# Bias of a fused adapter kernel as 32 rows of the slot products, and the first weight chunk in two transfers

## What is computed

```
y    = x @ W.T + b + 2 * (x @ A[slot].T) @ B[slot]
base = y @ W_base.T + b_base
top2, sel = top_k(y @ W_router.T, 2);  w = softmax(top2) spread over the 8 experts
h    = y @ A_e.T  for every expert e (rank 16)
out  = x + base + 2 * sum_e w_e * (h_e @ B_e)
```

## Time and profile before

| what | value |
|---|---|
| median of three executions | 66.52 us |
| the profiled execution, time | 66.64 us |
| the profiled execution, span from first to last instruction | 64.9 us |
| TensorE matmuls, busy | 61.1 us (94%), 422 matmuls |
| VectorE busy | 36.9 us (57%) |
| ScalarE busy | 22.9 us (35%) |
| GpSimd busy | 17.1 us (26%) |
| granted TensorE clock, mean over the span | 1.0 of full |
| read from memory, written | 7.37 MB, 2.10 MB |

### The profile page before, as it was taken

The page is one execution under the profiler, slowest core; times in us unless marked ns, Lnnn a source line. Parts: engine busy times, 40 slices in busy tenths (PEclk is TensorE's granted clock), DMA queues, the critical chain, the costliest instruction groups (busy, mean ns, idle before and its releaser), DMA issues.

```text
span 64.9 us, 1174 instructions
## 1 busy us (share of the span) xinstructions
PE 61.1 (94%) x422; PEld 60.2 (93%) x422; DVE 36.9 (57%) x105; ACT 22.9 (35%) x46; POOL 17.1 (26%) x29
## 2 busy tenths in 40 slices
PE   5989999999999999999999999999999999999920
PEld 5969999999999999989999999999999999999910
DVE  0057959999899685126805675012768255956040
ACT  0669078606999898054121100020201131020000
POOL 6700000000799997759360000011000000000000
PEclk9999999999999999999999999999999999999999
DMA  0899998303899305155659997500044000033513
GB/s 0 222 358 353 402 407 267 115 5 96 225 316 374 128 6 130 37 130 126 146 90 399 351 375 282 200 0 0 0 171 154 9 0 0 0 121 121 229 48 127
DMA packets 6025, 10.57 MB, mean 163 GB/s; under 512 B 755, under 2 KB 2547, under 8 KB 6020
## 3 DMA queue, kind: packets, MB, share of 16 engines
q1 hardware_dynamic: 5730, 10.17, 47.1%
q10 hardware_dynamic: 290, 0.33, 1.5%
HBM read 7.37 MB, written 2.10 MB: 146 GB/s over the span
## 4 chain that ended last, share of the span: by engine, by line
PE 89%; DMA 4%; ACT 1%; DVE 1%; DVEq 0%; issue 0%
PE ps L693 26%; PE ps L601 23%; PE ps L705 19%; PE ps L753 8%; PE ps L662 5%; DMA wt<-w_chunks 4%; PE ps L728 2%; PE ps L733 2%; PE ps L739 1%; PE ps L716 1%; ACT wt_hi L352 1%; DVE xn L554 1%; DVEq L71 0%; PE ps L672 0%
## 5 line engine op out<-in xcount | busy, mean ns | idle before, releaser
L693 PE MATMUL ps<-am,x_hi 128*128 128x384 f32 x64 | 16.6, 340 | 0.0
L705 PE MATMUL ps<-bm,x_hi 128*128 128x280 f32 x64 | 13.0, 297 | 0.0
L693 PEld LDWEIGHTS ps<-am,x_hi 128*128 128x128 f32 x64 | 11.4, 188 | 0.0
L693 PE MATMUL ps<-am,x_lo 128*128 128x384 f32 x32 | 10.8, 338 | 0.0
L319 POOL TENSOR_TENSOR x_lo<-xt,x_hi 128x512 fp32r<-128x512 f32 x8 | 10.8, 1361 | 0.0
L705 PEld LDWEIGHTS ps<-bm,x_hi 128*128 128x128 f32 x64 | 10.1, 189 | 0.0
L705 PE MATMUL ps<-bm,x_lo 128*128 128x280 f32 x32 | 9.3, 290 | 0.0
L554 DVE TENSOR_TENSOR xn<-ps,xn 128x280 f32<-128x280 f32 (+1 forms) x16 | 6.1, 418 | 2.7 <-PE ps L753 2.6
L601 PE MATMUL ps<-wt_hi 128*128 128x280 f32 (+1 forms) x32 | 7.0, 316 | 0.2 <-ACT wt_hi L352 0.2
L601 PE MATMUL ps<-wt_lo,wt_hi 128*128 128x280 f32 (+1 forms) x32 | 7.0, 314 | 0.0
L326 POOL CAST am<-as_hl 128x128 fp32r<-128x128 f32 x8 | 2.9, 373 | 14.1 <-PE ps L693 14.1
(11 more groups left out here) (74 smaller groups left out, 99.4 us busy)
## 6 DMA issues: line engine op xcount, KB each, us to landing
xt<-x_t SPq DMA_DIRECT2D x4, 512.0 KB, 6.5
xn<-x_n SPq DMA_DIRECT2D x4, 512.0 KB, 5.5
out_n<-xn SPq DMA_DIRECT2D x7, 256.0 KB, 2.1
wt<-w_chunks SPq DMA_DIRECT2D x2, 582.0 KB, 6.2
g_st<-g_hl SPq DMA_DIRECT2D x12, 81.0 KB, 2.1
ab<-adapters SPq DMA_DIRECT2D x8, 64.0 KB, 2.7
wt<-w_chunks SPq DMA_DIRECT2D x1, 326.0 KB, 4.2
wt<-w_chunks SPq DMA_DIRECT2D x2, 128.0 KB, 3.0
```

The source lines that it names most:

```text
L693: last = mm(a_bank(b)[:, 0:R + WA], v[:, p, i, tok], am[:, i, level, at:at + R + WA], start=(i == 0 and n == 0), stop=False, skip_group_ch ...
L705: mm(b_bank(b)[:, 0:QB], v[:, p, i, tok], bm[:, i, level, :], start=(i == 0 and n == 0), stop=False, skip_group_check=True)
```

## The change

1. Chunk 0 comes in two transfers: SP's queue brings all 512 stationary columns, ScalarE's queue all 652 moving ones. ScalarE rounds the stationary columns in two instructions of 256; VectorE's rounding of columns 0 to 255 is gone, and its remainder of the 512 stationary columns stands ahead of that of the last 368 moving ones. TensorE does all four high x high products of the first 280 columns, and then the four high x low ones.
2. The two matmuls with the ones are gone, and with them the matrix of ones, its rounding on GpSimd, and both splits around them. `bsum` is summed over partitions further: 64 rows to 32 (with `b_base`, which comes as row 0 of a 32-row input padded with zeros), 32 rows in place, then a transfer moves rows 16 to 31 to partitions 0 to 15 (`moved`), and VectorE adds them (`folded`). Sixteen rows are left; they are split in high and low, and stand as rows 96 to 127 of `g_st`, which now has 128 rows. Two transfers bring them for pair 0 ahead of the rest, two for the pairs 1 to 3.
3. Pair 0 (and 2) has banks 2 and 3 for `routed` and 4 and 5 for `plain`, pair 1 (and 3) banks 0 and 1, 6 and 7. Block 0's first products wait for the remainders of M row block by row block, not for all.
4. Order: `slots_routed(0)` stands behind `routed(3)`; `weighted_transpose(0)` behind `plain(1)`, no longer next to `stack_transpose(1)`; `plain(2)` ahead of the experts of blocks 0 and 1; ScalarE and VectorE follow (`stack_t(1)` ahead of `weighted_hi(0)`, `stack(1)` ahead of `choose(0)`).
5. The rounding of `x` for pairs 2 and 3 is in two instructions per pair and not in one.

```diff
-W0_PIECES = [slice(D // 2, D), slice(0, D // 2), slice(D, D + QB), slice(D + QB, CB)]
+W0_PIECES = [slice(0, D), slice(D, CB)]
-GK = CROW + 4
+GK = CROW + 2 * NC
...
-            for n in (0, 1):
-                sp.dma_start(wt[:, 0, W0_PIECES[n]], w[:, 0, W0_PIECES[n]]).then_inc(w0_in[n], 16)
+            sp.dma_start(wt[:, 0, W0_PIECES[0]], w[:, 0, W0_PIECES[0]]).then_inc(w0_in[0], 16)
...
-            sp.wait_ge(bb_hi_done, 1)
-            spread(CROW, bb_hl[:, 0:1, :])
-            sp.wait_ge(bb_lo_done, 1)
-            spread(CROW + 1, bb_hl[:, 1:2, :])
+            sp.wait_ge(quarter_done, 2)
+            sp.dma_start(moved, bsum[NC:QP]).then_inc(moved_in, 16)
...
-                    sp.wait_ge(c_hi_done, 2)
-                    sp.wait_ge(c_lo_done, 2)
+                    for i, ready in enumerate((c_hi_done, c_lo_done)):
+                        sp.wait_ge(ready, 1)
+                        sp.dma_start(g_st[CROW + i * NC:CROW + (i + 1) * NC, 0, :].bitcast(F32),
+                                     c_hl[:, i, :].bitcast(F32)).then_inc(gst_in[0], 16)
                     for i in range(2):
-                        spread(CROW + 2 + i, c_hl[:, i:i + 1, :])
+                        sp.dma_start(g_st[CROW + i * NC:CROW + (i + 1) * NC, 1:PAIRS, :].bitcast(F32),
+                                     c_hl[:, i:i + 1, :].bitcast(F32).to_broadcast([NC, PAIRS - 1, WC])
+                                     ).then_inc(cst_in, 16)
...
-            for n in (2, 3):
-                act.dma_start(wt[:, 0, W0_PIECES[n]], w[:, 0, W0_PIECES[n]]).then_inc(w0_in[n], 16)
+            act.dma_start(wt[:, 0, W0_PIECES[1]], w[:, 0, W0_PIECES[1]]).then_inc(w0_in[1], 16)
             act.wait_ge(w0_in[0], 16)
-            for i in (2, 3):
-                c = slice(i * P, (i + 1) * P)
+            for c in (slice(D // 2, D), slice(0, D // 2)):
                 hi(wt_hi[:, 0, c], wt[:, 0, c]).then_inc(w0_hi_done, 1)
...
+                if i == 2:
+                    dve.wait_ge(bbase_in, 16)
+                    dve.wait_ge(halves_done, 1)
+                    nc.vector.tensor_tensor(upper[0:QP], bsum[QP:HP], bb[QP:HP], ALU.add).then_inc(quarter_done, 1)
+                    dve.wait_ge(quarter_done, 1)
+                    nc.vector.tensor_tensor(bsum[0:QP], bsum[0:QP], upper[0:QP], ALU.add).then_inc(quarter_done, 1)
...
+            dve.wait_ge(moved_in, 16)
+            nc.vector.tensor_tensor(bsum[0:NC], bsum[0:NC], moved, ALU.add).then_inc(folded, 1)
...
-            for s, c in enumerate(COLS):
-                last = mm(ps[:, C_BANK + s, 0:c.stop - c.start], ones_r[:], bsum_st[:, c], start=True, stop=True)
-            last.then_inc(c_done, 1)
...
+                    if b == 0 and i != 1:
+                        pe.wait_ge(m_lo_done, 2 * max(i + 1, 2))
...
             routed(2, range(2, KB))
+            routed(3)
             slots_routed(0)
-            routed(3)
             plain(0)
-            weighted_transpose(0)
             stack_transpose(1)
             plain(1)
+            weighted_transpose(0)
             slots_plain(0)
             slots_plain(1)
             slots_routed(1)
+            plain(2)
             experts_block(0)
             experts_block(1)
-            plain(2)
```

More of the change, by code:

```diff
@@ L48 @@
 CB = CH + 4
+QP = HP // 2
+NC = (P - 6 * R) // 2
 NT = NE + NE * R
@@ L115, in build @@
         hw_flat = hw[:].rearrange("p a t c -> p (a t c)")
-        upper, bb = hw_flat[0:HP, 0:WC], hw_flat[HP:HP + 1, 0:WC]
+        upper, moved = hw_flat[0:HP, 0:WC], hw_flat[0:NC, 0:WC]
         hw_hi = sb("hw_hi", [P, NB, P], F32R)
@@ L120, in build, with first_a, first_b @@
         ident = sb("ident", [P, P])
-        ones = sb("ones", [P, P])
-        ones_r = sb("ones_r", [P, P], F32R)
         iota = sb("iota", [P, NE])
         ps = ctx.enter_context(nc.psum_tensor("ps", [P, 8, 512], F32))
-        G_BANK, C_BANK = 0, 2
-        def first_bank(p):
-            return 0 if p % 2 else 4
+        G_BANK = 0
+        def first_a(p):
+            return 0 if p % 2 else 2
+        def first_b(p):
+            return 6 if p % 2 else 4
         def a_bank(b):
-            return ps[:, first_bank(b // 2) + b % 2, :]
+            return ps[:, first_a(b // 2) + b % 2, :]
         def b_bank(b):
-            return ps[:, first_bank(b // 2) + 2 + b % 2, :]
+            return ps[:, first_b(b // 2) + b % 2, :]
         def x_rounded(p, n):
-            return 2 * p + n + 1 if p < 2 else 3 + p
+            return 2 * p + n + 1
         def rt_at(b):
@@ L301, in _ @@
             nc.gpsimd.memset(ident[:], 0.0).then_inc(id_zero, 1)
-            nc.gpsimd.memset(ones[:], 1.0).then_inc(const, 1)
             nc.gpsimd.memset(h_stack[:], 0.0).then_inc(id_zero, 1)
@@ L311, in _ @@
                            allow_small_or_imprecise_dtypes=True).then_inc(const, 1)
-            pool.wait_ge(const, 1)
-            nc.gpsimd.tensor_copy(ones_r[:], ones[:]).then_inc(ones_rounded, 1)
             def x_split(p, n):
@@ L374, in x_high @@
                 act.wait_ge(x_in[p], 16)
-                step = 2 if p < 2 else KB
-                for k in range(0, KB, step):
-                    hi(x_hi[:, p, k:k + step, :], xt[:, p, k:k + step, :]).then_inc(x_hi_done, 1)
+                for k in range(0, KB, 2):
+                    hi(x_hi[:, p, k:k + 2, :], xt[:, p, k:k + 2, :]).then_inc(x_hi_done, 1)
             w_high(1)
@@ L418, in weighted_hi @@
                 hi(hw_hi[:, 2 * p:2 * p + 2, :], a_scratch(p)).then_inc(hw_hi_done, 1)
-            for p in range(PAIRS):
+            stack_t(0)
+            shares(0)
+            stack_t(1)
+            weighted_hi(0)
+            shares(1)
+            weighted_hi(1)
+            for p in range(2, PAIRS):
                 stack_t(p)
@@ L491, in _ @@
                 lo(g_hl[:, 1, c], ps[:, G_BANK + s, 0:c.stop - c.start], g_hl[:, 0, c]).then_inc(g_lo_done, 1)
-            for s, c in enumerate(COLS):
-                dve.wait_ge(c_hi_done, s + 1)
-                lo(c_hl[0:1, 1, c], ps[0:1, C_BANK + s, 0:c.stop - c.start],
-                   c_hl[0:1, 0, c]).then_inc(c_lo_done, 1)
+            dve.wait_ge(c_hi_done, 1)
+            lo(c_hl[:, 1], bsum[0:NC], c_hl[:, 0]).then_inc(c_lo_done, 1)
             dve.wait_ge(bt_hi_done, 1)
@@ L561, in _ @@
             split(0)
+            stack(1)
             choose(0)
             weigh(0)
-            stack(1)
+            split(1)
             weighted_lo(0)
-            split(1)
             choose(1)
```

87 lines of the change are left out of this document (27 added, 60 removed).

## The result

The changed kernel takes **69.09 us** (median of 6 runs, 68.84 to 70.35) against 66.88 (66.47 to 67.40) for the kernel before on the same chip: 1.031 times, interval 1.026 to 1.037. That is 2.2 us slower, where 66.5 us was forecast with a range up to 66.85.

The account below looks back on a forecast made before the run. TensorE, busy 94% of the span, was taken as the bound. Terms +0.39 - 0.30 - 0.15 + 0.05 = -0.01 us against the profiled 66.64; from the runs' median, 66.52, this gives 66.5 us, range 66.15 to 66.85.

Parts of the forecast that it names:

- upper bound of the landing: Chunk 0's moving columns land at 4.60 us at the latest, with the last of the four old pieces, bytes being equal.
- Start of M: M's first products: later start, closed hole and one restart, +0.63 - 0.34 + 0.10 = +0.39 us.
- the lower bound: Chunk 0's landing at 4.26 us: longer runs 0.16 sooner, and 73 KB more in the slow first 0.65 us, another 0.18.
- the term +0.63 of the later start: TensorE starts M at 4.76 us (landing 4.40 + 0.36) instead of 4.13: +0.63 us.
- the moving part lands last: Slower rival at M's start: chunk 0's moving columns land at 4.6 to 4.9, total +0.2 to +0.5, 66.85 us; chance 0.19.
- The term -0.34 + 0.10 for the hole: The 0.34 us hole in M's first four products closes, except 0.10 for a restart after a wait.
- The early rival: Faster rival at M's start: chunk 0 lands at 4.2 or before, total -0.2 to -0.3, about 66.25 us; chance 0.26.
- The clock: Slower rival: after the longer pause TensorE runs M's first chunk at 1.2 GHz, 68 to 70 us; chance 0.04.
- The ones, the slot products, the transposes: TensorE: two matmuls go, -0.30 us; hole at the first slot products closes, -0.15; transposes set apart, +0.05.
- The `x` loads for the output: They leave SP's queue 1.5 us later because of the new transfers and are still early: 0.
- The fold: Bias additions on VectorE, 0.82 us by the nearest row, and their transfers are all covered: 0.

Follow-up runs that it names:

- e13: The changed kernel with chunk 1 issued only when the stationary part of chunk 0 is in: 68.64 us, one execution.
- e5: The changed kernel, unaltered, run again beside others on one chip: 69.70 us (67.57 to 70.29).
- e3: The changed kernel with 50 filling matmuls ahead of M for 28: 67.59 us, ratio 1.0094 to the kernel before.
- e14: The changed kernel with 43 filling products ahead of M for 28: 67.64 us, ratio 1.0131 to the kernel before.
- e12: The changed kernel with ScalarE's moving transfer cut at 280 columns, SP's whole, second time: 66.86 us (66.53 to 68.87, 13 runs).
- e1: The changed kernel with the old start of M (four transfers, old roundings and order of first products): 66.96 us, ratio 0.9996 to the kernel before.
- e6: The changed kernel with ScalarE's moving transfer cut at 280 columns, SP's whole, first time: 68.29 us (66.82 to 68.68, 4 runs).
- e15: The changed kernel with ScalarE's moving transfer cut at 280 columns and 35 filling products for 28: 67.08 us (66.59 to 68.19, 12 runs).
- e8: The same file as e1 (changed kernel with the old start of M), run later: 66.92 us, ratio 0.9988 to the kernel before.
- e11: The same file as e1 (changed kernel with the old start of M), third time, as control: 66.89 us, ratio 0.9976 to the kernel before.
- e4: The kernel before with 12 filling matmuls ahead of M for 28, transfers untouched: 67.92 us, ratio 1.0147.
- e7: The changed kernel with SP's stationary transfer cut in two, ScalarE's whole: 69.63 us (68.24 to 69.81).

## Why the prediction was wrong

Two steps failed: the upper bound of the landing, and M's length, which was taken at the full clock although the start moved behind a longer pause.

**Start of M: wrong, the first step that failed.** The landing was put between 4.26 and 4.60 us and taken as 4.40; it was 4.80 and 4.98, in four other executions of two transfers 4.83 to 5.29. The upper bound rested on "the bytes are the same", but the same bytes came more slowly: 464 KB are in from 1.75 to 3.70 us (0.65 x 156 + 1.3 x 279), for 542 KB before. The fewer and longer rows did help in the first 0.65 us, by 28 KB and not by the 73 of the lower bound (101 KB for 73), and then lost 107 KB in the 1.3 us behind it (279 GB/s for 361). The engines' unequal ends (e13) are another part; why they come more slowly there stays open. For the term +0.63 of the later start, 1.42 was measured. The rival "the moving part lands last" had the sign, but its mechanism is worth 0.2 to 0.4 us (e13), and the stationary part was last in four of five profiles, which the prediction held to be "no later than the moving one". The term -0.34 + 0.10 for the hole was right: 0.26 against 0.24.

The early rival did not come either. The Trainium skill ("DMA: Bandwidth & Descriptors", section "Anatomy of one DMA — SWDGE (gpsimd) path") has its figures for another issuing path; the estimate of 4.1 us worked out from them is 0.7 to 0.9 us short of the trace here.

**The clock: the second step, priced as a rival and given too small a chance.** The rival named the pause, and had 0.04; the sum itself had nothing for it. It is the larger loss: 1.27 us of M's length in the first profiled execution and 2.4 in e5 (17.16 for 14.74), and nine of ten executions lie where e3 and e14, with the pause shortened, have none. The chance rested on a granted clock of 1.00 in all stretches; but that column also reads 1.00 where the starts show half pace (e12). And the filling products of the kernel before told of it:

```profile
0.78 3.15 PE L597 MATMUL ps<-const-bfloat16-1.0 128*128 128x128 bf16 x28 [0.78 <-PEq L841]
```

From the first start, 0.78, to the last, 3.62, they are 0.105 apart, or 1.2 columns a nanosecond, where M's dense products have 280 columns in 0.128, 2.2 a nanosecond. So the clock rises only about when M starts, which the forecast could have read: a start that moves is a start with the clock in doubt.

**The ones, the slot products, the transposes: right as a sum.** -0.30 - 0.15 + 0.05 = -0.40 was forecast, -0.49 measured in the changed kernel; the distances at the slot products are dense. The gain also holds in e1, e6 and e15, where G starts at 19.2 us or later; in e8, where it starts at 18.84, it is gone.

**The `x` loads for the output: wrong, at no cost in this kernel.** The prediction had them 1.5 us later and "still early". They leave SP's queue at 37.00 us for 32.21, which against G's start is 2.1 us later, and VectorE waits 0.97 us for them ahead of `finish(0)` (40.59). TensorE loses nothing by it in the changed kernel, and 0.25 us in e11.

**The fold: right for this kernel, for a reason not seen.** The two additions took 0.82 each, as taken from the row of 64 partitions, and block 2 did not wait. But that was so because M was late and GpSimd idle, which is luck. With M at its old time they take up to 1.9 each, and the term 0 becomes up to +0.4 (e8). The sum had looked at what VectorE's queue delays and not at who else is at work.

**Why the profiled execution came out 2.2 us above the forecast sum**: +0.8 for the landing, +1.5 for the clock (1.27 for the -0.24 expected of M's length), -0.1 for the rest. Without the clock it would still have left the range: e3 and e14 stand at 67.6 us.

## What to carry to other kernels

The first transfers are not priced by bytes over rate: what counts is when the slowest engine has its last row, and fewer, longer transfers made that 0.4 to 0.7 us later here though the bytes were the same. A start that moves later has a second price, the clock of TensorE after the pause; before a head is delayed, read the distances of the filling products for the pace, and fill the pause or price M at both paces. And an operation that gains a place on one engine should be looked at beside what the neighbour engine does at that time, not only in its own queue.

## What the runs showed of the hardware

- After a pause of 0.75 to 1.8 us behind the filling products, TensorE's pace in the next 3 to 6 us is either that of 2.4 or that of 1.2 GHz, in executions of one file (e6 and e12: 66.82 and 68.80 us). In all four traces where it was 1.2 from M's start (e4, e5, e12, e13), it had not yet risen when the pause began. With more filling products the changed kernel has no execution above 68.5 in ten (e3 and e14), for nine in ten without. In the changed kernel's first profile the clock was granted in full first, and fell at 6.90, 1.35 us after work had started again.
- VectorE's additions with both operands in SBUF took 0.82 us alone and up to 1.81 to 1.91 beside GpSimd's subtractions of 1.3 us; the remainders of 280 columns with one operand in PSUM kept their 0.43 to 0.45 beside the same subtractions. The Trainium skill ("SBUF — State Buffer", section "Who interferes with whom") has it so: a VectorE instruction with two SBUF inputs and a GpSimd instruction that reads SBUF exclude each other, and the second one waits. By that rule, the trace agrees: 0.82 + 1.3 is the ceiling, and 1.91 is below it.
- Cutting ScalarE's transfer brought the untouched one of SP's queue forward by 0.7 us or more (4.12 to 4.25 in three traces, for 4.98 to 5.29 in five). Cutting SP's brought ScalarE's to 4.37, for 4.80 to 5.25. e13 shows that long rows end unevenly over the engines; why shorter rows on one queue bring the other forward was not settled.
- The table load of ScalarE (1.28 us) goes where the first instruction that needs it waits: one more wait ahead of it put it on the critical path (e7).
